# The experts' second product as three rounded products, with its operands split per tile on three engines

## The chip, the cores and the metric

One core of one Trainium2 chip runs the whole program. The metric is the time of one execution on the device in microseconds (us). A TensorE clock of 1.0 in the profile is its full 2.4 GHz.

## The reference, cut to what matters

The program computes two layers over 2 x 512 tokens of width 256. The first layer multiplies a selective scan with a mixture of experts, the second multiplies an attention with a layer of signs. The change is in the mixture of experts, whose reference is:

```
router = xt @ gate_w.T
probs, idx = jax.lax.top_k(router, K)          # K = 2 of E = 8 experts
for e in range(E):
    h = jax.nn.silu(xt @ fc1_w[e].T) * (xt @ fc2_w[e].T)    # 704 hidden units
    y = y + comb[:, e:e + 1] * (h @ proj_w[e].T)
```

The last line's product, `h @ proj_w[e].T`, is what the change makes in another way.

## The kernel before, in words

The 2048 pairs of a token and an expert are sorted by expert into NJ = 23 tiles of 128 rows, each for one expert. For tile j, GpSimd gathers the rows (`xg`), TensorE transposes them (`turn_x`, called X), ScalarE copies them to `xgT`. TensorE then makes the hidden values in three parts: H1 (the first product's 512 units, bank 0), H2 (the second product's, bank 1) and H3 (the remaining 192 of both, bank 2). ScalarE applies silu into `sil` after H1 and after H3; VectorE multiplies into `hE` (128 x 768, two buffers). `project(j)`, called P(j), then makes the tile's output from `hE` and the `proj_w` columns of `wm` (five blocks of 128 units) and `ptl` (the sixth), all in plain float32. VectorE scales the result by the router's weight into `y_row`, and GpSimd scatters that to DRAM. The hidden units are on the partitions, so P(j) sums six matmuls of 128 x 128 by 256 columns in bank 3.

Meanwhile the same engines run the selective scan in 8 chunks: F(c) on TensorE and two exponentials on ScalarE (`decays`), C(c) on TensorE, four copies `dx` on ScalarE (`skips`), products `mix` and `c_dec` on GpSimd (`mixes`), Y(c) on TensorE (`scan_back`), the state, `gate` and `y_lo` on VectorE, `y_hi` on ScalarE, and O(c) on TensorE (`out_rows`).

The order of both is written by hand in `side_by_side()`: a list of (place, engine, operation, number), sorted by place. Tile j has the places from 4j on, chunk c those from `CHUNK_AT[c]` = 3 + 11.5c. Each engine executes its operations strictly in that order and waits at the head of its queue on semaphores. So P(j-1) at place 4j + 3.1 stands between H3(j) and H1(j+1) on TensorE. SyncE loads the weights of a tile into one of three slots: `expert_rows(j)`, and `expert_back(j)` for the `proj_w` columns, which waits for P(j-3) to end.

The selective scan's last product in `out_rows` already has the form that the change brings to P(j): `split3` makes one product from three of type float32r (a rounded float32, here "the rounded format"): low part by high, high by low, high by high.

Of the kernel before, what the change touches and what calls it, by code (L numbers as in the profile page):

```python
# [175 lines left out]
def layered_kernel(nc, x, params, consts, select, rope, w_in, w_out, w_moe, w_moe_tail, w_qkv, w_o, w_sign, out):  # L176
# [4 lines left out]
    with ctx:  # L181
# [260 lines left out]
        wcen_ready, wsign_ready, sign_ready, sign_full, ab_ready, g1_ready, mask_ready, o_zero = sems(  # L442
            "wcen_ready wsign_ready sign_ready sign_full ab_ready g1_ready mask_ready o_zero")

        k_scaled, turns_full, turns_ready, rp4_ready, wqhi_done, wqlo_done, wohi_done, wolo_done, twice_in = sems(
            "k_scaled turns_full turns_ready rp4_ready wqhi_done wqlo_done wohi_done wolo_done twice_in")
# [228 lines left out]
        def _(dve):  # L675
# [270 lines left out]
            def centre_signs():  # L946

                dve.wait_ge(l1_in, 32)
                for i, (s, at) in enumerate(((0, 0), (1, 0), (1, HD // 2))):
# [4 lines left out]
                for m in range(KC):
                    TS(wcen[:, m, :], wsg[:, m, :], wst[:, m, 1:2], None, ALU.subtract).then_inc(wcen_ready, 1)
                TT(ab[:, :], cols("alpha"), cols("bias"), ALU.mult).then_inc(ab_ready, 1)
# [1073 lines left out]
```

## Time and profile before

| | |
|---|---|
| median of 3 runs | 753.35 us (749.12 to 753.63) |
| the profiled execution, its own time | 748.34 us |
| its span, first to last instruction | 746.5 us |
| mean granted TensorE clock | 0.993 |
| experts and scan side by side | about 66 to 299 us of the span |
| P(0) to P(22), records of L1734 | 276, from 79.3 to 296.8 us |

The page's first part gives each engine's busy time over the span. In the timeline, records of one line that follow each other are merged: `x10` are ten records, the number before the engine is the time from the first's start to the last's end. A float32 matmul is two records. A bracket tells how long the engine was idle before and who released it. Because matmuls are pipelined, the start of the next group is what tells when a group let go of the engine.

### The profile page before, as it was taken

How to read it: one execution, taken by the hardware profiler on the slowest of the kernel's cores; microseconds unless marked ns; L12 is line 12 of the kernel's file. 1: busy time of each engine (PE TensorE's matmuls, PEld its weight loads, DVE VectorE, ACT ScalarE, POOL GpSimd, SP SyncE). 2: the span in 40 equal slices, each digit the busy share in tenths (PEclk: the TensorE clock that was granted, in tenths of full speed). 3: DMA queues.
4: the chain of work that ended last, by engine and by line, in shares of the span. 5: the costliest groups of instructions: out<-in, count | busy, mean ns of one | idle time of the engine just before them, and what ended most of it. 6: DMA issues, size and time to landing. Idle time of an engine off the chain costs nothing.

```text
span 746.5 us, 13408 instructions
## 1 busy us (share of the span) xinstructions
PE 688.0 (92%) x4447; PEld 598.2 (80%) x4448; DVE 510.5 (68%) x1072; ACT 442.0 (59%) x1075; POOL 385.2 (52%) x434
## 2 busy tenths in 40 slices
PE   2999999999999999699879999999999999999976
PEld 2887998989889898587668888888888878787864
DVE  7483556434333245897878878888888888887765
ACT  4435343332341432448786787778877788878772
POOL 1403342432224312235765797777877788777540
PEclk9899999999999999999999999999999999999999
DMA  8165877787778755226533332343324423242011
GB/s 293 44 217 170 286 240 241 252 261 229 247 234 251 214 170 163 43 76 191 147 109 79 93 82 65 95 93 83 85 65 102 93 66 87 58 110 58 1 29 57
DMA packets 108453, 102.25 MB, mean 137 GB/s; under 512 B 51104, under 2 KB 78688, under 8 KB 108256
## 3 DMA queue, kind: packets, MB, share of 16 engines
q1 hardware_dynamic: 106272, 95.62, 44.8%
q0 software_dynamic: 2112, 5.77, 2.4%
q8 instruction: 36, 0.59, 0.3%
q14 instruction: 33, 0.27, 0.1%
HBM read 69.24 MB, written 11.14 MB: 108 GB/s over the span
## 4 chain that ended last, share of the span: by engine, by line
PE 65%; DVE 20%; ACT 6%; issue 5%; POOL 2%; DMA 1%; SPq 1%; DVEq 0%; ACTq 0%
PE bank L1700 14%; PE bank L1734 8%; PE bank L1556 7%; PE bank L1873 5%; DVE p_lo L1071 3%; PE bank L1840 3%; DVE o_rest L1080 3%; PE bank L1560 3%; DVE nmax L1062 3%; PE bank L1561 3%; PE bank L1562 3%; PE bank L1841 2%; DVE q_mix L1028 2%; DVE q_mix L1029 2%; PE bank L1884 2%
## 5 line engine op out<-in xcount | busy, mean ns | idle before, releaser
L1518 POOL TENSOR_TENSOR prob<-prob,rinv 128x128 f32<-128x128 f32 (+3 forms) x256 | 176.6, 722 | 89.2 <-DVE rinv L1067 89.2
L1322 ACT ACTIVATE prob<-bank,nmax 128x512 f32<-128x512 f32 (+3 forms) x256 | 133.2, 526 | 42.3 <-DVE nmax L1062 30.7
L1071 DVE TENSOR_TENSOR p_lo<-bank,p_hi 128x512 fp32r<-128x512 f32 x160 | 109.5, 685 | 58.0 <-ACT p_hi L1329 55.9
L1329 ACT ACTIVATE p_hi<-bank 128x512 fp32r<-128x512 f32 x160 | 95.4, 596 | 44.1 <-PE bank L1556 43.1
L1700 PEld LDWEIGHTS bank<-xgT,wm 128*128 128x128 f32 x920 | 108.7, 192 | 4.5 <-issue 2.9
L1700 PE MATMUL bank<-xgT,wm 128*128 128x128 f32 x920 | 111.3, 275 | 0.5 <-ACT xgT L1234 0.5
L1840 PE MATMUL bank<-kT,qT 128*128 128x512 f32 (+3 forms) x256 | 83.4, 331 | 19.8 <-ACT prob L1322 15.3
L1556 PE MATMUL bank<-cst,prob 128*128 128x128 f32 x640 | 96.6, 273 | 3.2 <-ACT prob L1322 2.5
L1062 DVE TENSOR_REDUCE nmax<-bank 128x1 f32<-128x512 f32 (+2 forms) x192 | 91.3, 502 | 2.8 <-PE bank L1843 2.6
L1873 PE MATMUL bank<-p_lo,v_parts 128*128 128x256 f32 (+3 forms) x288 | 91.7, 341 | 0.1
L1491 POOL DMA_INDIRECT y_rows<-y_row,to_row x21 | 22.8, 1084 | 118.2 <-DVE y_row L931 92.5
L1556 PEld LDWEIGHTS bank<-cst,prob 128*128 128x128 f32 x640 | 73.2, 141 | 5.2 <-ACT prob L1322 2.6
L1840 PEld LDWEIGHTS bank<-kT,qT 128*128 128x128 f32 x256 | 48.1, 188 | 33.9 <-ACT prob L1322 26.6
L1841 PE MATMUL bank<-kT,qT 128*128 128x512 f32 (+3 forms) x256 | 74.4, 321 | 0.0
L1873 PE MATMUL bank<-p_hi,v_parts 128*128 128x256 f32 (+3 forms) x288 | 74.2, 304 | 0.0
L1259 ACT ACTIVATE sil<-bank 128x512 f32<-128x512 f32 x23 | 13.7, 597 | 75.9 <-PE bank L1700 75.9
L971 DVE TENSOR_TENSOR hE<-sil,bank 128x512 f32<-128x512 f32 x23 | 15.8, 687 | 57.5 <-PE bank L1700 40.6
L1734 PE MATMUL bank<-wm,hE 128*128 128x256 f32 x230 | 53.5, 379 | 1.2 <-DVE y_low L936 1.2
L1873 PEld LDWEIGHTS bank<-p_lo,v_parts 128*128 128x128 f32 x288 | 52.1, 190 | 0.3 <-issue 0.3
L1873 PEld LDWEIGHTS bank<-p_hi,v_parts 128*128 128x128 f32 x288 | 52.4, 190 | 0.0
L1322 ACT ACTIVATION_READ_ACCUMULATOR prob<-bank,nmax 128x1 f32 x256 | 51.2, 200 | 0.0
L1841 PEld LDWEIGHTS bank<-kT,qT 128*128 128x128 f32 x256 | 48.2, 188 | 2.9
(310 smaller groups left out, 1517.9 us busy)
## 6 DMA issues: line engine op xcount, KB each, us to landing
wm<-in_w_moe SPq DMA_DIRECT2D x23, 1280.0 KB
wm<-in_w_moe SPq DMA_DIRECT2D x23, 640.0 KB, 5.1
qT<-q_hi SPq DMA_DIRECT2D x124, 64.0 KB, 2.0
qT<-q_lo SPq DMA_DIRECT2D x124, 64.0 KB, 2.0
wo_twice<-wo_hi SPq DMA_DIRECT2D x32, 128.0 KB, 2.5
k_exp<-k_rows SPq DMA_DIRECT2D x56, 64.0 KB, 2.0
wtl<-in_w_moe_tail SPq DMA_DIRECT2D x46, 64.0 KB
y_rows<-gate SPq DMA_DIRECT2D x1, 2048.0 KB, 13.8
```

Source lines behind the costliest of these rows:

```text
L1062: ins = vec.tensor_reduce(out=nmax[:, i % 2, h, j:j + 1], in_=bk[:, at:at + (j + 1) * P], op=ALU.max, axis=AX.X, negate=True)
L1071: TT(p_lo[:, b_, :], bank[2 + b_ % 2][:, :], p_hi[:, b_, :].bitcast(F32), ALU.subtract).then_inc(plo_done, 1)
L1322: ins = actv(prob[:, i % 2, h, POFF[j]:POFF[j] + (j + 1) * P], bk[:, at:at + (j + 1) * P], ACT.Exp, bias=nmax[:, i % 2, h, j:j + 1], accum ...
L1329: actv(p_hi[:, b_, :], bank[2 + b_ % 2][:, :], ACT.Copy).then_inc(phi_done, 1)
L1491: pool.indirect_dma_start(out=y_rows, out_offset=bass.IndirectOffsetOnAxis(ap=to_row[:, n:n + 1], axis=0), in_=y_row[:, n % 2, :], in_offs ...
L1518: ins = GT(seg, seg, rinv[:, i % 2, k, j:j + 1].to_broadcast([P, (j + 1) * P]), ALU.mult)
L1556: return nc.tensor.transpose(dst, src, ident)
L1700: ins = mm(dst, w(c), xgT[:, u, c, :], start=c == 0, stop=c == KC - 1)
L1734: ins = mm(bank[3][:, 0:C], hE[:, u, i * P:(i + 1) * P], wm[:, s, i, PJ:WM] if i < FULL else ptl[:, s, :], start=i == 0, stop=i == HC - 1)
L1840: mm(dst, qs, kT[:, b, 0, 0:n], start=(h, j, at) == SCORES[k][0], stop=False)
L1841: mm(dst, qs, kT[:, b, 1, 0:n], start=False, stop=False)
L1873: ins = mm(bank[4 + h][:, x:y], vs, p[:, b_, at + x - j * P:at + y - j * P], start=first and (h, j) in ((0, 0), (1, 2)), stop=end and (h, ...
```

## The change

P(j) is made of three products of the rounded format: low part of `hE` by high part of the weights, high by high, high by low. Four operations per tile are new:

- hU (ScalarE): `hE_hi`, the rounded copy of the tile's 128 x 768 `hE`. It waits until P(j-1) has ended, since `hE_hi` has one buffer.
- hL (VectorE): `hE_lo` = `hE` - `hE_hi`, 128 x 768.
- pU (ScalarE): `pj_hi`, the rounded copy of the tile's weights, 128 x 1280 and 128 x 256.
- pL (GpSimd): the low parts, written over the weights in `wm` (`wm_lo`), in pieces of 512, 512 and 256 columns, and `ptl_lo`, 256 columns.

`hE`, `hE_hi`, `hE_lo`, `pj_hi` and `ptl_lo` have one buffer each. Some semaphores are merged to make room for three new ones; each wait keeps its meaning.

```
+            z += [(at + 3.6, "ACT", "hU", j), (at + 3.7, "DVE", "hL", j), (at + 4.2, "ACT", "pU", j), (at + 4.3, "POOL", "pL", j)]
...
-                    if n > 1:
-                        dve.wait_ge(row_full, n - 1)
-                    TT(hE[:, u, 0:4 * P], sil[:, 0:4 * P], bank[1][:, :], ALU.mult).then_inc(hE_done, 1)
+                    if n > 0:
+                        dve.wait_ge(hlo_done, n)
+                    TT(hE[:, 0:4 * P], sil[:, 0:4 * P], bank[1][:, :], ALU.mult).then_inc(hE_done, 1)
...
+                elif op == "hL":
+                    dve.wait_ge(upper_done, 2 * n + 1)
+                    TT(hE_lo[:, :], hE[:, :], hE_hi[:, :].bitcast(F32), ALU.subtract).then_inc(hlo_done, 1)
...
+                elif op == "hU":
+                    act.wait_ge(hE_done, 2 * n + 2)
+                    if n == 0:
+                        act.wait_ge(ones_ready, 5)
+                    else:
+                        act.wait_ge(row_full, n)
+                    actv(hE_hi[:, :], hE[:, :], ACT.Copy).then_inc(upper_done, 1)
+                elif op == "pU":
+                    s = n % 3
+                    act.wait_ge(back_in[s], 32 * (n // 3 + 1))
+                    actv(pj_hi[:, 0:FULL, :], wm[:, s, :, PJ:WM], ACT.Copy)
+                    actv(pj_hi[:, FULL, :], ptl[:, s, :], ACT.Copy).then_inc(upper_done, 1)
...
+                elif op == "pL":
+                    s = n % 3
+                    gp_.wait_ge(upper_done, 2 * n + 2)
+                    for lo, hi in ((0, 2), (2, 4), (4, FULL)):
+                        GT(wm_lo[:, s, lo:hi, PJ:WM], wm[:, s, lo:hi, PJ:WM], pj_hi[:, lo:hi, :].bitcast(F32), ALU.subtract)
+                    GT(ptl_lo[:, :], ptl[:, s, :], pj_hi[:, FULL, :].bitcast(F32), ALU.subtract).then_inc(pjlo_done, 1)
...
+                pe.wait_ge(upper_done, 2 * j + 2)
+                pe.wait_ge(hlo_done, j + 1)
                 for i in range(HC):
-                    ins = mm(bank[3][:, 0:C], hE[:, u, i * P:(i + 1) * P], wm[:, s, i, PJ:WM] if i < FULL else ptl[:, s, :],
-                             start=i == 0, stop=i == HC - 1)
+                    ps = slice(i * P, (i + 1) * P)
+                    mm(bank[3][:, 0:C], hE_lo[:, ps], pj_hi[:, i, :], start=i == 0, stop=False)
+                    mm(bank[3][:, 0:C], hE_hi[:, ps], pj_hi[:, i, :], start=False, stop=False)
+                pe.wait_ge(pjlo_done, j + 1)
+                for i in range(HC):
+                    ins = mm(bank[3][:, 0:C], hE_hi[:, i * P:(i + 1) * P], wm_lo[:, s, i, PJ:WM] if i < FULL else ptl_lo[:, :],
+                             start=False, stop=i == HC - 1)
                 ins.then_inc(row_full, 1)
```

GpSimd's queue around tile 9, where chunk 3 asks for `mix` and `c_dec`. Before (the scatter of tile 7's rows, the gather for tile 12, the scatter of tile 8's, the gather for tile 13, then the scan):

```order
L1491 DMA y_rows<-y_row,to_row 4992x256
L1457 DMA xg<-xn_rows,from_row 128x256
L1491 DMA y_rows<-y_row,to_row 4992x256
L1457 DMA xg<-xn_rows,from_row 128x256
L1466 TENSOR_TENSOR mix<-within,cbm 128x512
L1468 TENSOR_TENSOR c_dec<-since,CT 128x512
```

The same place now, from the scatter of tile 8's rows on:

```order
L1521 DMA y_rows<-y_row,to_row 4992x256
L1481 DMA xg<-xn_rows,from_row 128x256
L1515 TENSOR_TENSOR wm_lo<-wm,pj_hi 128x2x256 x2
L1515 TENSOR_TENSOR wm_lo<-wm,pj_hi 128x256
L1516 TENSOR_TENSOR ptl_lo<-ptl,pj_hi 128x256
L1490 TENSOR_TENSOR mix<-within,cbm 128x512
L1492 TENSOR_TENSOR c_dec<-since,CT 128x512
```

The four subtractions pL(9) now stand ahead of the scan's two products. Chunks 0, 1 and 2 have the same order (pL of tiles 0, 3 and 6).

ScalarE's queue between the silu after H3(6) and the next tile, where chunk 2 has its exponentials and `dx`. Before:

```order
L1217 ACT_TABLE_LOAD
L1217 ACTIVATE within<-bank 128x512
L1218 ACTIVATE since<-bank 128x512
L1226 ACTIVATE dx<-xs,par 128x128 x4
L1259 ACT_TABLE_LOAD
L1259 ACTIVATE sil<-bank 128x512
L1234 ACTIVATE xgT<-bank 128x256
```

Now:

```order
L1229 ACT_TABLE_LOAD
L1229 ACTIVATE within<-bank 128x512
L1230 ACTIVATE since<-bank 128x512
L1284 ACTIVATE hE_hi<-hE 128x768
L1238 ACTIVATE dx<-xs,par 128x128 x4
L1271 ACT_TABLE_LOAD
L1271 ACTIVATE sil<-bank 128x512
L1288 ACTIVATE pj_hi<-wm 128x1280
L1289 ACTIVATE pj_hi<-ptl 128x256
L1246 ACTIVATE xgT<-bank 128x256
```

hU(6), which waits for P(5), now stands ahead of `dx`, the table load and the silu of H1(7), and pU(6) behind that silu.

TensorE's queue from the last third of P(6) on, now:

```order
L1771 MATMUL bank<-wm_lo,hE_hi 128x256 x5
L1771 MATMUL bank<-ptl_lo,hE_hi 128x256
L1696 MATMUL bank<-mix,x_dt 128x128
L1698 MATMUL bank<-c_dec,state 128x128
```

Y(2) (`mix`, `c_dec`) still follows P(6) at once, as before, and H1(8) stands behind it.

## Rows read from the trace of the kernel before

**Rows 1.** The page, part 1: busy time of each engine, share, count.
```profile
PE 688.0 (92%) x4447; PEld 598.2 (80%) x4448; DVE 510.5 (68%) x1072; ACT 442.0 (59%) x1075; POOL 385.2 (52%) x434
```
**Rows 2.** Tile hE: the line that scales each tile's result after P(j).
```profile
L931 DVE TENSOR_SCALAR y_row<-bank,tab x21: 475/484/484, 82.1 to 283.1; 128x256 f32<-128x256 f32 x21
```
**Rows 3.** Timeline (start, us, engine, line): P(8), H1(10), c_dec, Y(3), H1(11).
```profile
159.78 2.32 PE L1734 MATMUL bank<-wm,hE 128*128 128x256 f32 x10
...
162.38 1.95 PE L1700 MATMUL bank<-xgT,wm 128*128 128x128 f32 x16
...
166.87 1.28 POOL L1468 TENSOR_TENSOR c_dec<-since,CT 128x512 f32<-128x512 f32 x1
...
168.41 0.46 PE L1666 MATMUL bank<-mix,x_dt 128*128 128x128 f32 x2 [0.73 <-POOL c_dec L1468]
...
173.72 1.95 PE L1700 MATMUL bank<-xgT,wm 128*128 128x128 f32 x16
```
**Rows 4.** Timeline: O(0), twelve rounded matmuls of 256 columns, and what follows.
```profile
93.08 0.36 PE L1560 MATMUL bank<-w_out_hi,y_lo 128*128 128x256 f32 x1
93.28 0.28 PE L1561 MATMUL bank<-w_out_lo,y_hi 128*128 128x256 f32 x1
...
94.59 0.38 PE L1556 MATMUL bank<-cst,xg 128*128 128x128 f32 x2
```
**Rows 5.** Timeline of ACT: silu after H1(8), copies of 256, 512 and 1024 columns.
```profile
145.13 0.60 ACT L1259 ACTIVATE sil<-bank 128x512 f32<-128x512 f32 x1 [6.46 <-PE bank L1700]
145.62 0.38 ACT L1234 ACTIVATE xgT<-bank 128x256 f32<-128x256 f32 x1
145.89 0.63 ACT L1206 ACTIVATE y_hi<-gate 128x512 fp32r<-128x512 f32 x1
...
292.47 1.04 ACT L1252 ACTIVATE wv_hi<-wv 128x1024 fp32r<-128x1024 f32 x1
```
**Rows 6.** Timeline of POOL: two subtractions into the rounded format.
```profile
296.19 2.38 POOL L1483 TENSOR_TENSOR wv_lo<-wv,wv_hi 128x1024 fp32r<-128x1024 f32 x1 [11.34 <-DVE xs L985]
300.36 1.27 POOL L1486 TENSOR_TENSOR wk_lo<-wk,wk_hi 128x512 fp32r<-128x512 f32 x1 [1.80 <-DVE xs L985]
```
**Rows 7.** Timeline of PE: C(2), P(6), Y(2), H1(8), P(7).
```profile
132.12 0.38 PE L1649 MATMUL bank<-CT,BT 128*128 128x128 f32 x2
...
132.78 1.95 PE L1700 MATMUL bank<-xgT,wm 128*128 128x128 f32 x16
...
137.91 2.32 PE L1734 MATMUL bank<-wm,hE 128*128 128x256 f32 x10
...
140.50 0.38 PE L1666 MATMUL bank<-mix,x_dt 128*128 128x128 f32 x2
...
143.15 1.95 PE L1700 MATMUL bank<-xgT,wm 128*128 128x128 f32 x16
...
148.28 2.32 PE L1734 MATMUL bank<-wm,hE 128*128 128x256 f32 x10
```
**Rows 8.** Timeline of ACT: table load before a silu, and the four dx copies.
```profile
130.85 1.27 ACT L1226 ACTIVATE dx<-xs,par 128x128 f32<-128x128 f32 x4
132.14 1.28 ACT L1259 ACT_TABLE_LOAD   x1
```
**Rows 9.** Timeline: DVE after H3(0); PE when it lets go of P(0).
```profile
72.89 0.29 DVE L975 TENSOR_TENSOR hE<-sil,bank 64x128 f32<-64x128 f32 x1
...
81.90 1.95 PE L1700 MATMUL bank<-xgT,wm 128*128 128x128 f32 x16
```
**Rows 10.** Timeline of PE: the end of P(21), then P(22).
```profile
292.59 0.59 PE L1734 MATMUL bank<-ptl,hE 128*128 128x256 f32 x2
294.38 2.40 PE L1734 MATMUL bank<-wm,hE 128*128 128x256 f32 x10 [1.19 <-DVE y_low L936]
```
**Rows 11.** Timeline: a product on POOL and one on DVE that start together.
```profile
114.69 1.05 POOL L1447 TENSOR_TENSOR decay_in<-cst,dts 128x512 f32<-128x512 f32 x1
114.73 1.57 DVE L904 TENSOR_TENSOR state<-state,since 128x512 f32<-128x512 f32 x1 [0.92 <-PE bank L1668]
```

More of the change, by code:

```diff
@@ L196, in layered_kernel @@
         x_tok = sb("x_tok", [P, NT, C])
+        xnT_at = (nc.sbuf_base + 31) // 32 * 32
         xnT = sb("xnT", [P, KC, T])
@@ L264, in layered_kernel @@
         ssm = first("ssm", [P, NCH, TAPS - 1 + SEQ])
+        route_at = first.at
         route = first("route", [P, NT, E])
@@ L324, in layered_kernel @@
         rp4 = turns[:, :, :].rearrange("p i (t h d) -> p i t h d", t=TB, h=4)
+        idle = Map(xnT_at)
+        pj_hi = idle("pj_hi", [P, HC, C], F32R)
+        ptl_lo = idle("ptl_lo", [P, C], F32R)
+        hE_hi = Map(route_at)("hE_hi", [P, HC * P], F32R)
         tiles = Map(scan.at)
@@ L327, in layered_kernel @@
         sil = tiles("sil", [P, HC * P])
-        hE = tiles("hE", [P, 2, HC * P])
+        hE = tiles("hE", [P, HC * P])
+        hE_lo = tiles("hE_lo", [P, HC * P], F32R)
         y_row = tiles("y_row", [P, 2, C])
@@ L335, in layered_kernel @@
         ptl = weights("ptl", [P, 3, C])
+        wm_lo = Map(weights.at)("wm_lo", [P, 3, FULL, WM], F32R)
         wm = weights("wm", [P, 3, FULL, WM])
@@ L436, in layered_kernel @@
         row_out = [sem(f"row_out{i}") for i in range(2)]
-        pad_zero, xg_full, xgT_ready, hid_full, sil_done, hE_done, row_full, row_taken = sems(
-            "pad_zero xg_full xgT_ready hid_full sil_done hE_done row_full row_taken")
+        upper_done, hlo_done, pjlo_done, xg_full, xgT_ready, hid_full, sil_done, hE_done, row_full, row_taken = sems(
+            "upper_done hlo_done pjlo_done xg_full xgT_ready hid_full sil_done hE_done row_full row_taken")
         mixed, gated = sems("mixed gated")
         sg_ready, back_full, x_ready, q_first, second_ready = sems("sg_ready back_full x_ready q_first second_ready")
[L442 to L446, printed above, removed]
+        signs_ready, wsign_ready, sign_ready, sign_full, g1_ready, mask_ready, o_zero = sems(
+            "signs_ready wsign_ready sign_ready sign_full g1_ready mask_ready o_zero")
+        k_scaled, turns_full, turns_ready, wqhi_done, wqlo_done, wohi_done, wolo_done, twice_in = sems(
+            "k_scaled turns_full turns_ready wqhi_done wqlo_done wohi_done wolo_done twice_in")
         v_full, v_copied, kx_full, kx_roped, kadd_done, k_in, khi_done, klo_done, vhi_done, vlo_done = sems(
@@ L879, in _ @@
             dve.wait_ge(pr_full, len(PROJS))
-            vec.memset(hE[0:TAIL, :, FULL * P:HC * P], 0.0).then_inc(pad_zero, 1)
+            vec.memset(hE[0:TAIL, FULL * P:HC * P], 0.0).then_inc(ones_ready, 1)
             def scan_front(c):
@@ L954, in centre_signs @@
                 for m in range(KC):
[L955 to L956 removed]
+                    TS(wcen[:, m, :], wsg[:, m, :], wst[:, m, 1:2], None, ALU.subtract).then_inc(signs_ready, 1)
+                TT(ab[:, :], cols("alpha"), cols("bias"), ALU.mult).then_inc(signs_ready, 1)
             for engine, op, n in side_by_side():
@@ L1406, in _ @@
             act.sem_inc(exp_done, 2)
-            act.wait_ge(ab_ready, 1)
+            act.wait_ge(signs_ready, 3 + KC + 1)
             attend(0, schedule("first"))
@@ L1728, in project @@
                 if j == 0:
-                    pe.wait_ge(pad_zero, 2)
+                    pe.wait_ge(ones_ready, 5)
                 pe.wait_ge(xgT_ready, min(j + 3, NJ))
@@ L1776, in _ @@
             sum_pair(3)
-            pe.wait_ge(rp4_ready, 3)
+            pe.wait_ge(signs_ready, 3)
             for i in range(3):
```

12 lines of the change are left out of this document (6 added, 6 removed).

## The prediction

> **What bounds the kernel now.** The page's first part has TensorE busy for 92% of the span and no other engine above 68% [rows 1]. In the stretch with the experts its timeline has almost no bracket: P, H1, X, H2, H3 and the scan's pieces follow each other, and the one long wait among P(8) to H1(11) is 0.73 us for `c_dec` [rows 3]. So a microsecond less on TensorE is a microsecond less in all, as long as nobody makes TensorE wait. The 21 scaled tiles lie 201.0 us apart from first to last, 10.05 us a tile [rows 2]. The shortest period is tile 6's: from 132.12, when TensorE lets go of P(5), to 140.50, when it lets go of P(6), 8.38 us [rows 7]; tile 3 has the same. I call T(j) the moment at which TensorE lets go of P(j).
>
> **The matmuls: -8.7 us.** P(j) takes 162.38 - 159.78 = 2.60 us now [rows 3]. The new form has the pattern of O(0), rounded, 256 columns: twelve in 94.59 - 93.08 = 1.51 us, and behind the first 1.31 / 11 = 0.119 us each [rows 4]. So the first twelve take 1.51, the last six 0.71, together 2.22 us: 0.38 less per tile, 8.7 us for 23. Bounds: if each group of six pays the start again, 2.26 (7.8 us); if none does, 18 x 0.119 = 2.14 (10.6 us). This is all that the change can win.
>
> **The new chain.** hU(j) can't start before T(j-1). From there to T(j), in a tile with nothing in the way:
> - hU, 768 columns. ScalarE copies 256, 512 and 1024 columns in 0.38, 0.63 and 1.04 us and starts the next one some 0.1 us before the end [rows 5], so 768 take 0.82. From T(j-1) + 0.2, it is done at 1.0.
> - Next in its queue is the silu of H1(j+1), which needs TensorE's H1: in tile 8, H1 begins at 143.15 and the silu at 145.13, 1.98 later [rows 7, 5]. It gives way after 0.49.
> - pU: 1280 columns, 1.17 by the same slope, then 256, 0.38. Done at 1.98 + 0.49 + 1.55 = 4.02.
> - pL: GpSimd takes 1.27 for 512 and 2.38 for 1024 columns [rows 6], 0.0022 a column; 512, 512, 256, 256 take 1.24 + 1.24 + 0.68 + 0.71 = 3.87. With 0.08 to start, done at 7.97.
> - TensorE sees it 0.26 later (as `c_dec`, which ends at 166.87 + 1.28 = 168.15 for Y(3) at 168.41 [rows 3]) and makes the last six in 0.71: T(j) = T(j-1) + **8.95 us**.
>
> The weights are no part of it: they are asked for after P(j-3), two tiles earlier. hL, about 0.95, is done before pU.
>
> A tile with a period of over 9.33 (8.95 + 0.38) hides the chain and wins its 0.38; most do, at a mean of 10.05. These don't, worked out in order of the queues. "Loss" is against the period less 0.38:
> - **Tile 0, 3.2.** hU(0) waits for `hE` (73.18 [rows 9]) and stands ahead of chunk 0's table load and exponentials, so these end some 1.5 later; the silu of H1(1) comes at 77.75, pU at 78.2 to 79.8, pL until 83.75, the end of P(0) at 84.7 instead of 81.90.
> - **Tile 3, 1.2.** A table load of 1.28 [rows 8] behind hU moves the silu to 2.3: 9.25 against 8.00.
> - **Tile 6, 2.4.** hU to 1.0, the four `dx` to 2.2, the table load to 3.5 [rows 8], silu, pU to 5.5, pL to 9.4: 10.4 against 8.00.
> - **Tile 7, 3.4.** `mix` and `c_dec` stand behind pL(6) and are done 2.5 after it, at T(5) + 12.0. Y(2) follows P(6) at once [rows 7] and so waits 1.8. Y(2) takes 2.65 (140.50 to 143.15), H1(8) is behind it, and the whole chain behind H1(8): 1.8 + 2.65 + 8.95 = 13.4, against 10.37 - 0.38 = 9.99.
> - **Tile 9, 5.0.** hU, table load, silu and pU to 4.35, pL to 8.3, `mix` and `c_dec` to 10.8. Y(3) is due at T(8) + 5 and starts at 11.05; it takes 2.71, and P(9) 2.22 behind it: 16.0, against 173.72 - 162.38 - 0.38 = 10.96 [rows 3].
> - **Tiles 12, 15, 16, 19, 2.9 in all.** Worked out in the same way from their places in the timeline: GpSimd's scatter, `mix` and gather ahead of pL make the chain 9.35, 11.1 and 9.3 in tiles 12, 15, 16; in tile 19 `y_hi` stands ahead of hU, 10.3. Their periods less 0.38 are shorter by 0.3, 0.8, 0.6 and 1.2.
> - **Tile 22, 4.0.** Nothing but P(22) is left, so the chain stands free, without the H1: 0.2 + 0.82 + 1.55 + 0.08 + 3.87 + 0.26 + 0.71 = 7.5. Now 294.38 + 2.60 - (292.59 + 0.43) = 3.96 [rows 10], less 0.38 is 3.6.
> - **Collisions, 1.2.** A product of two SBUF tensors on VectorE that starts with one on GpSimd takes 1.57: until GpSimd's ends at 115.74, and 0.56 more [rows 11]. `y_lo` for O(3) and O(4) now meets pL; I take 0.6 for each.
>
> Sum of the losses 3.2 + 1.2 + 2.4 + 3.4 + 5.0 + 2.9 + 4.0 + 1.2 = 23.3; less 8.7 is **+14.6 us**. Behind the stage nothing hides it: the layer's sum needs P(22). Against the profiled execution's own 748.34 this is 763; against the median of 753.35 it is 768. The four known times lie in two pairs (748.3, 749.1; 753.4, 753.6), so I take **766**.
>
> A rule that speaks against the change: the Trainium skill, GPSIMD Engine Reference, section Key points, says that GpSimd contends with VectorE instructions of two SBUF inputs. By rows 11 that is one exclusion in a stretch; by the rule every one of hL, `y_lo`, the state's and the gate's products pays where it meets pL, and the sum would be that of the third case below.
>
> **The rivals.**
> 1. *The waits as worked out*: 0.60. Its own range, with the bounds of the matmuls and 20% on pL's length in eight places, is 758 to 775.
> 2. *A shorter chain.* If GpSimd's and ScalarE's copies of 128 x 1280 strided columns run 20% faster than the slope (it comes from two rows, rows 6), each of the eight losing places gives back about 0.9: +7, 757 to 762. 0.16. Against it: nothing in rows 5 or 6 is faster with more columns.
> 3. *The two engines exclude each other.* pL lasts 3.87 of each tile. Each chunk has three or four VectorE products of two SBUF tensors (`state`, `gate`, `y_lo`, and hL each tile); 8 chunks, each one such meeting of 0.9 in a chain that TensorE waits for: +7 more, 773 to 782. 0.15. Rows 11 speak for it, that most such products follow TensorE's and fall ahead of pL speaks against it.
> 4. *Faster.* The split ends before TensorE gets there, and the 8.7 stay: 742 to 748. The mechanism is the length of pL: the chain hides in the short tiles once it is below 8.00, so pL would have to be under 2.9 instead of 3.87, and for tile 9 it would have to end before T(8) + 2.4, where GpSimd hasn't yet the upper parts. The second can't be, so only the rest of it can. 0.09.
>
> A difference of 1% (7.5 us) is what can be told from none here. Above 760.9 lie all of the third case, nearly all of the first and a quarter of the second: slower 0.76; same 0.15; faster 0.09. The range for 8 in 10 is 755 to 778: it leaves out the fourth case, a bit of the low end and half of the third.
>
> **What would show it.** The rounded matmuls of P have starts 0.12 us apart. In most tiles P(j)'s second line waits for nobody; in tiles 0, 3, 6, 7, 22 TensorE idles before the line with `wm_lo`, with `ptl_lo`'s subtraction as releaser, and before Y(2) and Y(3) with `c_dec` as releaser, about 1.8 and 6 us. T(9) - T(8) is 16 instead of 11.3, T(22) - T(21) 7.5. pL is four operations of 3.9 us in all. The attention behind it keeps its length. I am wrong if pL takes clearly less, if the chain's start isn't T(j-1), or if VectorE's products stretch to 1.5 us by the dozen.

## The result and the profile after

The changed kernel takes **789.38 us** (median of 4 runs, 787.44 to 793.58) against 753.49 us of the kernel before in the same comparison. It is slower: the two medians stand 4.8% apart, and the ratio on record is 1.054 (95% interval 1.050 to 1.058). I had forecast slower, at 766 us, with a range from 755 to 778. The direction was right; the size was 23 us short. The profiled execution took 793.58 us, its span is 791.8 us.

The page's first part, which answers to [rows 1]:

```profile
PE 698.4 (88%) x4585; PEld 610.3 (77%) x4586; DVE 553.8 (70%) x1095; ACT 492.8 (62%) x1144; POOL 482.6 (61%) x526
```

TensorE's busy time went up by 10 us, although it has less to do: a busy microsecond is worth less where the clock is halved. The line that scales each tile's result starts 233.9 us apart from first to last, where it was 201.0 [rows 2]:

```profile
L940 DVE TENSOR_SCALAR y_row<-bank,tab x21: 472/484/485, 85.0 to 318.9; 128x256 f32<-128x256 f32 x21
```

TensorE lets go of P(22) at 336.8 us instead of 297.0, so 39.8 of the 45.3 us of span lie in this stage. (The two profiled executions are further apart than the medians, which differ by 36 us.) The rest lies behind the stage, which I had expected to keep its length: 455.0 us after T(22) instead of 449.5, with the same matmuls, at a mean granted clock of 0.98 instead of 1.00. In the traces of the experiments below it is 451 to 455 us, so most of this is a difference between single executions. Tile by tile (T(j) - T(j-1), in us; the others differ by at most 0.7 from before):

| tile | before | forecast | after |
|---|---|---|---|
| 0, T itself | 81.9 | 84.7 | 84.8 |
| 1 | 9.5 | 9.1 | 9.2 |
| **2** | 11.1 | 10.7 | **18.5** |
| 3 | 8.4 | 9.25 | 9.4 |
| 4 | 10.4 | 10.0 | 11.1 |
| 5 | 10.9 | 10.5 | 12.4 |
| 6 and 7 | 18.6 | 23.8 | 27.3 |
| 8 | 11.7 | 11.3 | 12.6 |
| 9 | 11.3 | 16.0 | 18.4 |
| 15 | 10.7 | 11.1 | 12.5 |
| **19** | 9.45 | 10.3 | **13.6** |
| 22, from T(21) | 4.0 | 7.5 | 8.9 |

**The matmuls and the chain are as worked out.** P(1) at the high clock, twelve and then six at a pitch of 0.12 us (columns: start, us from the first's start to the last's end, engine, line, what is written and read):

```profile
91.62 0.36 PE L1767 MATMUL bank<-pj_hi,hE_lo 128*128 128x256 f32 x1
91.82 0.28 PE L1768 MATMUL bank<-pj_hi,hE_hi 128*128 128x256 f32 x1
91.94 0.28 PE L1767 MATMUL bank<-pj_hi,hE_lo 128*128 128x256 f32 x1
...
93.17 0.85 PE L1771 MATMUL bank<-wm_lo,hE_hi 128*128 128x256 f32 x5
...
93.99 1.94 PE L1730 MATMUL bank<-xgT,wm 128*128 128x128 f32 x16
```

ScalarE's part behind T(3) = 121.83: hU 0.84 (estimate 0.82), the silu of H1(4) 1.98 behind T(3), pU 1.26 and 0.41 (estimates 1.17 and 0.38), done at T + 4.0:

```profile
122.08 0.84 ACT L1284 ACTIVATE hE_hi<-hE 128x768 fp32r<-128x768 f32 x1 [2.75 <-PE bank L1771]
123.81 0.60 ACT L1271 ACTIVATE sil<-bank 128x512 f32<-128x512 f32 x1 [0.88 <-PE bank L1730]
124.30 1.26 ACT L1288 ACTIVATE pj_hi<-wm 128x1280 fp32r<-128x1280 f32 x1
125.46 0.41 ACT L1289 ACTIVATE pj_hi<-ptl 128x256 fp32r<-128x256 f32 x1
```

**What was not in the sum: VectorE stands still beside pL.** VectorE and GpSimd around T(1) and in tile 2:

```profile
91.94 0.68 DVE L920 TENSOR_TENSOR dx<-bank,dx 128x512 f32<-128x512 f32 x1
92.65 2.77 DVE L921 TENSOR_TENSOR gate<-dx,gate 128x512 f32<-128x512 f32 x1
...
97.82 6.76 DVE L874 SCALAR_TENSOR_TENSOR xs<-ssm,par,xs 128x512 f32<-128x512 f32 x3
```
```profile
92.39 0.73 POOL L1516 TENSOR_TENSOR ptl_lo<-ptl,pj_hi 128x256 fp32r<-128x256 f32 x1
93.09 1.03 POOL L1471 TENSOR_TENSOR decay_in<-cst,dts 128x512 f32<-128x512 f32 x1
94.11 0.76 POOL L1458 TENSOR_SCALAR xs<-ssm,par 128x512 f32<-128x512 f32 x1
...
99.44 3.17 POOL L1515 TENSOR_TENSOR wm_lo<-wm,pj_hi 128x512 fp32r<-128x512 f32 x3
102.58 0.71 POOL L1516 TENSOR_TENSOR ptl_lo<-ptl,pj_hi 128x256 fp32r<-128x256 f32 x1
103.28 0.76 POOL L1458 TENSOR_SCALAR xs<-ssm,par 128x512 f32<-128x512 f32 x1
```

The gate product starts at 92.65 and ends at 95.42, which is 0.55 behind the end of GpSimd's *third* instruction in a row (94.11 + 0.76 = 94.87), not behind the one that it met. The taps' three products end at 104.58, again 0.54 behind the end of GpSimd's unbroken run (104.04); without a meeting they take 2.31 together. In [rows 11] I had read the same 0.56 behind a single instruction and priced a meeting by one instruction. `dx`, which reads PSUM, keeps its 0.68 while pL runs. Not every meeting lasts to the run's end. Beside runs of two or more GpSimd instructions, 14 VectorE instructions of the stage were stretched: three lasted to the end (this gate, the first tap, and the gate at 129.34 us) and took 10.1 us more than the same instructions elsewhere, eleven ended within the run and took 8.5 us more. In all, 20 instructions took 23.3 us more up to T(22), 13 of them 1.5 us or longer; in the kernel before it was two, with 1.1 us. That is the last sign that I had named ("stretch to 1.5 us by the dozen"). H2(3)'s and the residual's operations stand behind the taps in VectorE's queue, and TensorE behind those:

```profile
105.78 2.05 PE L1671 MATMUL bank<-decay_in,cst 128*128 128x512 f32 x2 [3.60 <-DVE sT L931]
107.62 1.91 PE L1672 MATMUL bank<-decay_in,ones 128*128 128x512 f32 x2
...
109.55 0.42 PE L1768 MATMUL bank<-pj_hi,hE_hi 128*128 128x256 f32 x1
109.76 0.41 PE L1767 MATMUL bank<-pj_hi,hE_lo 128*128 128x256 f32 x1
```

**And the clock.** Behind that wait the pitch is 0.21 instead of 0.12 us: TensorE runs at the lower of its two levels, 1.2 instead of 2.4 GHz. Busy time of the engines in stretches of the stage (the number before the last two is the granted clock, as a share of full speed):

```profile
core 0: us, PE busy (x) PEld busy (x) DVE busy (x) ACT busy (x) POOL busy (x), PEclk, DMA share, GB/s
66.00:102.00 36.00, 31.57 (x254) 29.21 (x253) 19.78 (x28) 19.28 (x39) 21.49 (x22) 1.00 0.71 218
102.00:113.00 11.00, 7.40 (x29) 5.19 (x28) 4.51 (x6) 3.71 (x7) 2.04 (x3) 0.69 0.42 131
...
191.00:204.00 13.00, 6.78 (x41) 6.34 (x42) 3.08 (x5) 0.24 (x2) 5.96 (x5) 0.74 0.35 113
204.00:301.00 97.00, 89.36 (x720) 83.03 (x718) 50.52 (x83) 52.89 (x96) 69.33 (x65) 1.00 0.75 235
...
328.00:338.00 10.00, 5.53 (x25) 5.25 (x25) 5.65 (x8) 4.34 (x7) 7.16 (x5) 0.60 0.37 122
```

The kernel before had 1.00 in the whole stretch from 66 to 300. Summed over short stretches up to T(22), TensorE's busy time times (1 - granted clock) is 11.7 us; I call this the low clock's share.

TensorE's waits up to T(22) (us in total, how often, the longest):

```profile
PE bank L1771 <- POOL ptl_lo L1516: 10.6, 9, 1.9
PE bank L1696 <- POOL c_dec L1492: 9.4, 3, 6.8
PE bank L1590 <- DVE y_lo L926: 7.5, 5, 2.6
PE bank L1671 <- DVE sT L931: 3.6, 1, 3.6
PE bank L1767 <- ACT pj_hi L1289: 2.7, 1, 2.7
```

All idle brackets of TensorE from 66 us to T(22) add up to 38.1 us; before, to 2.9. So the books nearly close: 38.1 - 2.9 + 11.7 - 8.7 = 38.2, against the 39.8 us by which T(22) is later. For the runs below the same sum, each with its own gain from the matmuls, holds within 1 us, except in e10 (1.8) and e5 (3.6) and where waits are filled, if it is counted from each run's own start of the stage: in ten of them (e3 to e7, v1 to v3, e9 and e12) this lies 1.6 to 2.0 us earlier, because less low clock stands ahead of it, so that their T(22) in the table flatters them by that much.

### The profile page after: what moved, and what is told of

It is laid out like the page before. It is cut to its first block, busy times and chain, and to the rows that moved or that the text cites. A ratio compares the mean times of both kernels' runs of the same rounds, so it can differ in the third digit from the quotient of the medians.

```text
span 791.8 us, 13914 instructions
## 1 busy us (share of the span) xinstructions
PE 698.4 (88%) x4585; PEld 610.3 (77%) x4586; DVE 553.8 (70%) x1095; ACT 492.8 (62%) x1144; POOL 482.6 (61%) x526
## 4 chain that ended last, share of the span: by engine, by line
PE 47%; DVE 24%; POOL 12%; issue 9%; ACT 6%; DMA 1%; SPq 1%; DVEq 0%; ACTq 0%; POOLq 0%
PE bank L1586 6%; PE bank L1730 5%; POOL wm_lo L1515 5%; PE bank L1910 5%; DVE p_lo L1083 3%; PE bank L1877 3%; PE bank L1590 3%; DVE o_rest L1092 3%; PE bank L1592 3%; PE bank L1591 3%; DVE nmax L1074 3%; PE bank L1878 2%; DVE q_mix L1040 2%; DVE q_mix L1041 2%; PE bank L1921 2%
## 5 line engine op out<-in xcount | busy, mean ns | idle before, releaser
L1730 PE MATMUL bank<-xgT,wm 128*128 128x128 f32 x920 | 112.9, 278 | 0.5 <-ACT xgT L1246 0.5
L1515 POOL TENSOR_TENSOR wm_lo<-wm,pj_hi 128x512 fp32r<-128x512 f32 (+1 forms) x69 | 77.9, 1158 | 38.0 <-ACT pj_hi L1289 37.9
L1521 POOL DMA_INDIRECT y_rows<-y_row,to_row x21 | 24.7, 1176 | 53.1 <-DVE y_row L940 49.9
L1284 ACT ACTIVATE hE_hi<-hE 128x768 fp32r<-128x768 f32 x23 | 19.3, 841 | 58.3 <-PE bank L1771 53.5
L1092 DVE SCALAR_TENSOR_TENSOR o_rest<-o_hi,minus,bank 128x512 fp32r<-128x512 f32 x64 | 47.1, 736 | 1.0 <-ACT o_hi L1365 1.0
```

Of the source, the lines that this page charges most:

```text
L1092: STT(out=to, in0=o_hi[:, b, m, :].bitcast(F32), scalar=minus[:, k:k + 1], in1=bank[4 + k][:, :], op0=ALU.mult, op1=ALU.add).then_inc(olo_ ...
L1515: GT(wm_lo[:, s, lo:hi, PJ:WM], wm[:, s, lo:hi, PJ:WM], pj_hi[:, lo:hi, :].bitcast(F32), ALU.subtract)
L1730: ins = mm(dst, w(c), xgT[:, u, c, :], start=c == 0, stop=c == KC - 1)
```

## The experiments

Three theories of the missing 23 us. **A, the exclusion:** VectorE's products stop beside pL, up to as long as GpSimd's run lasts, and TensorE behind them. **B, the length:** pL's time in the chain and in GpSimd's queue costs more than worked out. **C, the clock:** what TensorE's low clock costs, and whether it comes from TensorE's own waits or from the load beside it. The texts on record word their theories B and C for each run anew. Each ratio is to the kernel before, run with it on the same chip (748 to 750 us), with its 95% interval.

| run | us | ratio | T(22) | TensorE idle | low clock |
|---|---|---|---|---|---|
| before | 749 | | 297.0 | 2.9 | 0 |
| after | 789.4 | 1.054 | 336.8 | 38.1 | 11.7 |
| e1_low_on_dve | 785.5 | 1.048 (1.039 to 1.056) | 330.9 | 35.0 | 10.8 |
| e2_low_behind_scan | 790.7 | 1.055 (1.049 to 1.061) | 337.5 | 39.3 | 12.4 |
| e3_no_low_weights | 733.7 | 0.981 (0.976 to 0.987) | 280.0 | 12.9 | 0 |
| e4_before_plus_subtractions | 767.3 | 1.022 (1.015 to 1.029) | 311.5 | 14.6 | 3.4 |
| e5_one_operand | 800.0 | 1.068 (1.061 to 1.074) | 343.0 | 43.1 | 12.6 |
| e6_before_plus_one_operand | 767.7 | 1.024 (1.019 to 1.030) | 311.1 | 13.2 | 4.9 |
| v1_parts_first | 804.3 | 1.073 (1.067 to 1.079) | 347.3 | 45.8 | 17.6 |
| v2_parts_first_on_dve | 774.8 | 1.034 (1.028 to 1.040) | 319.3 | 28.7 | 7.1 |
| e7_tiny_memsets | 754.5 | 1.009 (1.007 to 1.012) | 300.2 | 14.6 | 2.6 |
| e8_before_plus_tiny_memsets | 751.0 | 1.004 (1.002 to 1.006) | 299.4 | 4.2 | 1.7 |
| e9_waits_filled | 792.3 | 1.058 (1.055 to 1.061) | 337.6 | | 2.6 |
| **e10_116_memsets** | 772.3 | 1.028 (1.022 to 1.034) | 318.0 | 26.2 | 5.0 |
| **e11_before_plus_116_memsets** | 756.6 | 1.009 (1.007 to 1.012) | 305.4 | 8.2 | 2.7 |
| e12_half_the_filling | 783.3 | 1.045 (1.040 to 1.050) | 328.7 | 24.7 | 3.4 |
| v3_out_later | 771.3 | 1.029 (1.024 to 1.034) | 318.1 | 27.3 | 7.1 |

### First four: the parts of the change

**e1_low_on_dve**, pL on VectorE:

```
-            z += [... (at + 4.3, "POOL", "pL", j)]
+            z += [... (at + 4.3, "DVE", "pL", j)]
```

> The changed kernel with the four subtractions of pL made by VectorE, at the same place in the order. Theory A, the exclusion: most of the 27 us by which the stage came out longer than worked out is VectorE standing still while GpSimd runs pL (gate's, taps' and xs' products of 2.8, 6.8 and 4.2 us), and what the half clock of TensorE costs behind such a stop. With GpSimd out of it no product of VectorE lasts longer than before the change, the chain gets shorter by some 2 us (VectorE does the four in about 1.9 us instead of 3.9) and mix and c_dec come as early as before: 750 to 765. Theory B, the chain itself with its queue on ScalarE: only the 2 us of the chain in the eight losing tiles come back, 770 to 780. Theory C, VectorE has no room for 23 x 1.9 us more in front of H2 and state: 775 or more, with VectorE named as releaser before H3 and Y.

785.5 us. The gate and `y_lo` are short again, but pL now waits for pU on VectorE at T + 4 with everything of the chunk behind it: TensorE waited 17.9 us for `y_lo` in seven places instead of 7.5 in five. Nor is the exclusion gone: pL's own subtractions, now on VectorE, met GpSimd's products of the scan (up to 2.52 us instead of 0.68, beside `mix` and `c_dec`). One cause had taken the place of another, so this run could not tell A from B; its own theory C (no room on VectorE, 775 or more) had the time, though TensorE waited before O and not before H3 and Y.

**e2_low_behind_scan**, pL at 4j + 6.1, behind `mix` and `c_dec`:

> The changed kernel with pL at place 4j+6.1 instead of 4j+4.3, so that in GpSimd's queue mix and c_dec of a chunk stand ahead of it. Theory A, the exclusion: the 1.7 and 6.8 us before Y(2) and Y(3) go, and what the low clock behind them costs, but pL still runs 4.2 us per tile beside VectorE and its products still stop, and P's last six wait longer in the tiles where mix is ahead: 778 to 792. Theory B, the order in GpSimd's queue is where the loss came from: 765 to 775.

790.7 us. The waits before Y fell from 9.4 to 1.6 us and came back before the last six matmuls (17.0) and before O (11.5). So a change of the order in GpSimd's queue alone gives nothing back.

**e3_no_low_weights**, no pL and no last six matmuls:

> The changed kernel without pL and without the last six matmuls of each P (the products with the weights' lower parts are left out). hU, hL and pU stay. The matmuls alone are 23 x 0.71 = 16.3 us less than in the changed kernel and 23 x 1.09 = 25 less than before. Theory A, the exclusion: no wait of more than a microsecond is left, 730 to 742. Theory B, the copies on ScalarE (2.4 us per tile ahead of exponentials and silus) carry a good part of the loss: 755 or more, with TensorE idle before H2, H3 or F for ScalarE.

733.7 us, 15 below before, where the matmuls alone are 25 less. hU, hL and pU thus cost about 10 us: idle time rose by about 10 us, of it 3.5 before O and 2.7 in tile 22 for `pj_hi`. The rest of the change's loss hangs on pL.

**e4_before_plus_subtractions**, the kernel before with pL's work beside it and nobody waiting for it:

```
+                    for lo, hi in ((0, 512), (512, 1024), (1024, 1280), (1280, 1536)):
+                        ins = GT(spare_low[:, lo:hi], x_flat[:, lo:hi], x_flat[:, lo + 256:hi + 256], ALU.subtract)
```

> The kernel before, and beside it four subtractions of GpSimd per tile at pL's place, of pL's sizes (512, 512, 256, 256 columns of float32, two SBUF operands, other data and an unused area), started by the silu of H1(j+1); nobody waits for them before the stage's end, so only the time they take on GpSimd and in its memory port is added. Theory A, the exclusion: VectorE's products stop behind them as in the changed kernel and TensorE behind VectorE, and mix and c_dec come later: 762 to 780, with single gate, taps or state products of 2 us and more. Theory B, it is the new chain (P waits for the parts) that costs: 753 to 758.

767.3 us: 18 to 19 us only because GpSimd is busy. The gate products took 1.27 us in the mean and `y_lo` 1.41 (before 0.72 and 0.69), and TensorE waited for both engines:

```profile
PE bank L1572 <- DVE y_lo L921: 6.8, 4, 3.6
PE bank L1678 <- POOL c_dec L1473: 6.1, 2, 4.5
```

That refutes the chain's half of theory B, since this kernel has no chain through pL. What GpSimd's queue costs by itself is told by e11 below: 7 of these 19 us.

### Second four: one operand, and another order

**e5_one_operand** and **e6_before_plus_one_operand**:

```
-  GT(wm_lo[...], wm[...], pj_hi[...], ALU.subtract)
+  pool.tensor_scalar(wm_lo[...], wm[...], w, b, ALU.mult, ALU.add)
```

> The changed kernel with pL as ten scalings of one SBUF operand each (256 or 128 columns by a scalar per partition, two of the 256 written to an unused area) that should take 3.6 to 4.0 us together, as its four subtractions do; the lower parts of the weights are thus replaced by scaled copies. The places, the waits and the queue are the same; only the second operand is gone. Theory A, the exclusion: VectorE's gate, taps, xs and y_lo keep their 0.7 us, the idle times before O (y_lo) and H2 (sT) go, and with them some of the low clock: 768 to 780. Theory B, pL's length and place in the queues alone: 785 to 793.

> The kernel before, and beside it per tile five scalings of 512 columns with one SBUF operand on GpSimd at pL's place (3.9 us together), where e4_before_plus_subtractions had four subtractions with two. Theory A, the exclusion: the 6.8 us of waiting for y_lo of that run go and what is left is mix and c_dec behind the new work, 6 us and less: 753 to 760. Theory B, GpSimd's time in the queue alone costs the 19 us of that run: 764 to 770.

Both misses for theory A (e6 fell in the range of its theory B). e5 did not hold pL's length: a scaling of 256 columns took 0.57 us, one of 128 up to 0.51, so pL had 5.3 us instead of 4.1, and the wait before the last six went from 10.6 to 25.3 us. It can't be read for or against A. e6 did hold it (0.80 us each) and cost the same as e4. Its trace shows why: one SBUF operand on GpSimd's side is enough. VectorE, then GpSimd:

```profile
186.31 4.20 DVE L923 TENSOR_TENSOR y_lo<-gate,y_hi 128x512 fp32r<-128x512 f32 x1
```
```profile
185.20 0.77 POOL L1499 TENSOR_SCALAR spare_too<-x_tok,par 128x512 fp32r<-128x512 f32 x1
185.95 3.00 POOL L1501 TENSOR_SCALAR spare_low<-x_tok,par 128x512 fp32r<-128x512 f32 x4
188.93 1.03 POOL L1454 TENSOR_TENSOR decay_in<-cst,dts 128x512 f32<-128x512 f32 x1
```

`y_lo` ends at 190.51, GpSimd's run of six instructions at 189.96: 0.55 apart again. Only my idea that the second operand of GpSimd matters fell.

**v1_parts_first**, pU ahead of the silu, hU behind it, `mix` ahead of pL:

```
+            z += [(at + 4.2, "ACT", "hU", j), (at + 4.3, "DVE", "hL", j), (at + 3.6 if j else 0.5, "ACT", "pU", j),
+                  ({0: 0.6, 3: 17.6, 6: 29.1, 9: 40.6}.get(j, at + 4.15), "POOL", "pL", j)]
```

> The changed kernel with another order: pU ahead of the silu of H1(j+1) and hU behind it, pL at 4j+4.15, tile 0's pU and pL already behind H1(0), and mix and c_dec of chunks 1 to 3 ahead of pL(3), pL(6) and pL(9). The chain from T(j-1) to T(j) is 0.2 + 1.55 + 0.08 + 3.87 + 0.26 + 0.71 = 6.7 instead of 8.95 us. If the chain and the queue are the greater part of the loss (10.6 us before wm_lo, 9.4 before Y, 3.2 in tile 0), 764 to 772 with almost no low clock left. If the exclusion and what the clock makes of it are, 776 to 788, since pL's 4.2 us beside VectorE stay.

804.3 us, the slowest of all, and worse than both expectations. The shorter chain starts pL while hU is still to come, so that hL meets pL in 13 of the 23 tiles:

```profile
L989 DVE TENSOR_TENSOR hE_lo<-hE,hE_hi 128x768 fp32r<-128x768 f32 x22 | 54.6, 2481 | 46.9 <-ACT hE_hi L1283 46.8
L875 DVE SCALAR_TENSOR_TENSOR xs<-ssm,par,xs 128x512 f32<-128x512 f32 x12 | 20.5, 1709 | 0.3
```

hL takes 2.48 us in the mean (0.95 alone), the taps 1.71 (0.75). TensorE waited 19.8 us for `y_lo` and 9.0 for `hE_lo`.

**v2_parts_first_on_dve**, the same with pL on VectorE:

> The order of v1_parts_first and pL on VectorE, ahead of hL. e1_low_on_dve had VectorE waiting for pU at T+4 with H2's product, state and y_lo behind it (17.9 us before y_lo); here pU is done at T+1.8, pL at T+3.7, hL at T+4.7, before H2's product is due. No exclusion, no late mix, no late silu: 745 to 757. Rival: VectorE, busy for 26 of 40 us then, still comes late with y_lo and state in the chunks: 765 or more.

774.8 us, so the rival: with pL and hL ahead of it `y_lo` is late (15.3 us in seven places). The exclusion that I had called gone is there too, in another place: gate, taps and `y_lo` keep their length, but the subtractions themselves have two SBUF operands and wait for GpSimd's `mix`, `c_dec` and `decay_in`. Twelve of them took 17 us more than alone. VectorE (the three take about 1.6 us alone), then GpSimd:

```profile
172.00 4.33 DVE L994 TENSOR_TENSOR wm_lo<-wm,pj_hi 128x512 fp32r<-128x512 f32 x3
```
```profile
173.54 1.28 POOL L1497 TENSOR_TENSOR mix<-within,cbm 128x512 f32<-128x512 f32 x1
174.77 1.26 POOL L1499 TENSOR_TENSOR c_dec<-since,CT 128x512 f32<-128x512 f32 x1
```

### Third: the length without long instructions

**e7_tiny_memsets** (where P's last six matmuls read `pj_hi`, so the low parts of the weights are left out) and **e8_before_plus_tiny_memsets**:

```
+                    for i in range(42):
+                        ins = pool.memset(unused[:, i:i + 1], 0.0)
+                    ins.then_inc(pjlo_done, 1)
```

> The changed kernel with pL as 42 memsets of 128 x 1 on GpSimd (0.10 us each where the trace has one alone, so about 4 us), and P's last six matmuls with the upper parts of the weights again (so the lower parts of the weights are left out). Queue, place and waits of pL stay and so does its length, but no instruction of it is longer than 0.1 us, so that VectorE can get in at any moment. Theory A, the exclusion (VectorE's products behind a long instruction or an unbroken run of GpSimd's are the idle times before O, 7.5 us, before tile 2's F, 3.6, and part of the low clock): gate, taps, y_lo and xs at 0.7 us, 770 to 778. Theory B, pL's length in chain and queue: 785 to 795. The run with one operand could not tell this, since its ten scalings took 5.4 us instead of 4.

> The kernel before, and beside it 42 memsets of 128 x 1 per tile on GpSimd at pL's place. Runs with four subtractions or five scalings there both came out 18 to 19 us over before, with gate and y_lo of VectorE at 1.25 us. Theory A: what VectorE loses there is the exclusion, by any long GpSimd instruction with one operand or two; with tiny ones only mix and c_dec are late (6 us of waits): 755 to 761. Theory B, queue occupancy alone: 765 to 770.

754.5 and 751.0 us, both below the expectation, since 42 memsets took 1.45 us in a row, not 4. They say something else: even with a pL of 1.45 us and no exclusion beside it the new form isn't faster than before.

**e10_116_memsets** and **e11_before_plus_116_memsets**, the same with 116:

> e7_tiny_memsets once more with 116 memsets instead of 42, since these took 0.034 us each and 1.45 together: 116 take 3.95 us, as pL's four subtractions do by themselves. The chain, the queue and the waits are thus those of the changed kernel, and no GpSimd instruction of pL is long. The lower parts of the weights are left out. Theory A, the exclusion: 767 to 775, with gate, taps, xs and y_lo at 0.7 us, no idle before tile 2's F, and the waits before the last six and before Y(2) and Y(3) that I had worked out (chain and queue), since what is left is the case that I had forecast, 766. Theory B, pL's length in chain and queue alone: 785 to 793.

> The kernel before with 116 memsets per tile on GpSimd at pL's place, 3.95 us that nobody waits for. With subtractions there it was 19 us slower, of which its trace had 6.1 us of waits for c_dec, 6.8 for y_lo and 3 of low clock. Theory A, the exclusion: the waits for c_dec stay and those for y_lo go: 755 to 760. Theory B, GpSimd's time alone: 765 to 770.

Both as theory A has it. 116 memsets take 3.8 to 3.9 us, pL's own length. e10 is 17 us below the changed kernel, and VectorE's gate and taps are back at their old means (total us, mean ns). `y_lo` is so only in part, 0.90 us (0.69 before, 1.05 in the changed kernel), because it also meets `decay_in` and GpSimd's tap:

```profile
L875 DVE SCALAR_TENSOR_TENSOR xs<-ssm,par,xs 128x512 f32<-128x512 f32 x12 | 9.0, 750 | 1.0 <-POOL xs L1459 0.7
L922 DVE TENSOR_TENSOR gate<-dx,gate 128x512 f32<-128x512 f32 x8 | 5.5, 692 | 0.3
```

In the changed kernel the same two were:

```profile
L874 DVE SCALAR_TENSOR_TENSOR xs<-ssm,par,xs 128x512 f32<-128x512 f32 x12 | 13.4, 1120 | 1.0 <-POOL xs L1458 0.7
L921 DVE TENSOR_TENSOR gate<-dx,gate 128x512 f32<-128x512 f32 x8 | 11.1, 1393 | 0.3
```

TensorE's waits in e10:

```profile
PE bank L1771 <- POOL unused L1515: 9.2, 9, 1.9
PE bank L1696 <- POOL c_dec L1493: 8.4, 3, 5.8
PE bank L1767 <- ACT pj_hi L1290: 2.7, 1, 2.7
PE bank L1590 <- DVE y_lo L927: 2.4, 2, 1.5
```

The chain's and the queue's waits are nearly as in the changed kernel (17.6 us instead of 20.0); the 3.6 us for `sT` are gone and those for `y_lo` fell from 7.5 to 2.4. Many tiles are those of the forecast: 10.7 in tile 2, 9.3 in tile 3, 10.4 in tile 5. Tiles 6 and 7 (25.6 instead of 23.8) and tile 9 (18.5 instead of 16.0) are longer than the forecast here too, so what they have above it isn't the exclusion beside pL. In e11 the same `y_lo` that took 4.20 us beside the scalings takes 0.68 in the middle of the memsets. VectorE, then GpSimd:

```profile
186.99 0.68 DVE L921 TENSOR_TENSOR y_lo<-gate,y_hi 128x512 fp32r<-128x512 f32 x1
```
```profile
185.78 3.78 POOL L1497 MEMSET spare_low<- 128x1 f32 x116
```

A memset reads nothing and is short, and these runs don't tell which of the two lets VectorE through. Nor does it let everything through: a copy `turns`, which took 0.41 us alone, took 2.26 us beside e10's memsets and 1.52 beside e11's, and ended 0.28 us behind each run. Of e4's 19 us, e11 keeps 7; TensorE's waits for `c_dec` are the same in both (6.1 and 5.8 us), so the other 12 come with the subtractions and not with GpSimd's time.

### The clock

**e9_waits_filled** and **e12_half_the_filling**, useless matmuls ahead of TensorE's longest waits (e9: 28, 48, 18, 20 and 12 of them; e12, shown here at the second place: 14, 27, 9, 8 and 6):

```
+                if c == 3:
+                    fill(27, 2 * 10 + 1)
                 pe.wait_ge(mix_ready, c + 1)
```

> The changed kernel with useless matmuls (128x128, float32, 0.12 us each at the high clock) in the waits of TensorE that stand before its low clock: 28 before chunk 1's F, 48 before Y(3), 18 before O(6), 20 before P(22) and 12 before its last six. If the half clock (12.1 us of busy time lost, by the windows of its trace) follows from TensorE standing idle, it stays at 2.4 GHz in tiles 2, 9, 20 and 22, and 6 to 8 us come back: 780 to 785. If it comes from the load of the other engines, the time is as before or longer by what the filling overshoots: 789 to 793.

> e9_waits_filled with half the filling, since each filling matmul was two passes of 0.118 us and the filling ran on for 2.8 us after chunk 1's F could have begun, and about 4 after Y(3) could: 14, 27, 9, 8 and 6 now. With the high clock F(1) to P(2) took 3.8 us there instead of 6.7, Y(3) to P(9) 4.8 instead of 6.3. If that is what the clock costs and nothing else is behind, 782 to 786; if the chain behind (the silu and pL of the next tile) sets the end whatever the clock is, 788 to 792.

e9 came out at 792.3 us: the filling ran on beyond the waits, because each of its float32 matmuls is two records of 0.12 us. Yet tile 2 took 18.1 us there instead of 18.5, although the filling ended about 2.5 us late: F(1) to the end of P(2) took 3.8 us at the high clock and 6.7 at the low one. With half of it, e12, 783.3 us: 6 us less than the changed kernel (the ratios' intervals only just meet; from each run's own start of the stage to T(22) it is 6.3 us), by nothing but matmuls that nobody needs. Three stretches of e12, around tiles 2, 9 and 22:

```profile
96.00:113.00 17.00, 16.49 (x136) 15.37 (x135) 12.63 (x16) 9.57 (x17) 8.80 (x10) 1.00 0.63 197
186.00:204.00 18.00, 16.02 (x136) 15.19 (x134) 8.48 (x13) 4.67 (x10) 11.03 (x10) 1.00 0.43 138
318.00:330.00 12.00, 9.40 (x80) 9.04 (x79) 8.04 (x13) 5.48 (x9) 8.14 (x7) 1.00 0.57 176
```

So in these stretches the low clock followed from TensorE's own idle time, not from the load beside it. Of the low clock's share of 11.7 us e12 removed 8.3, and 6 of them showed in the time; that the rest falls where another wait follows anyway is my reading and wasn't tested. Idle time isn't all that comes before a low clock: in the kernel before, the granted clock also fell to half at 26.0 us, while TensorE was busy with matmuls of 8 columns each and had not waited more than 0.5 us at a time since 13.3 us.

### Can the order give it back?

**v3_out_later**, v2 with O(c) 1.1 places later:

```
-        o = a + (9.5 if c + 1 < NT else 12.7)
+        o = a + (10.6 if c + 1 < NT else 12.7)
```

> v2_parts_first_on_dve (774.8 us) with the scan's O(c) 1.1 places later, at a + 10.6, so that TensorE has a product of a tile more to do before it needs y_lo. In that run the waits for y_lo were 15.3 us in seven chunks, up to 3.4 each. If they only came from O standing too early in TensorE's order, 760 to 766; if VectorE is late by as much as its load of 26 in 40 us makes it, the wait turns up again before H2, H3 or the next F: 770 to 776.

771.3 us. The wait for `y_lo` fell from 15.3 to 3.0 us and turned up again before P (`hE_lo`, 11.6 instead of 7.3) and before F (`sT`, 6.5 instead of 2.0): it is VectorE's load, with the stretched subtractions in it, not O's place. None of the versions tried beats the kernel before. As an estimate, the best that a hidden pL could give is e3 and the last six matmuls, 733.7 + 16.3 = 750 us, no better than before.

## Why the prediction was right and where it was wrong

- **Matmuls, -8.7: right.** P(1)'s first twelve took 1.50 us and its last six 0.82, against 1.51 and 0.71 worked out; in P(2), where the parts were there in time, the last six took 0.71.
- **The new chain, 8.95: right.** Tile 3 took 9.36 us against 9.25 worked out, T(0) came at 84.82 against 84.7. pL's own four operations took 3.9 us where nothing met them, 4.1 in the mean, up to 4.8 in tiles 9, 10 and 22.
- **The queue (tiles 7 and 9): right in place.** `c_dec` was the releaser before Y(2) and Y(3), with 1.69 and 6.78 us, where I had 1.8 and 6.
- **"Collisions, 1.2": the step that failed.** The mechanism was there, the term was mis-sized. The changed kernel without pL's part of it (e10) is at 772.3 us, so it costs 17 us: TensorE waits 11.9 us less there, ten times the 1.2, and the low clock's share is 6.7 us less. Of the 11.9, 8.7 are waits for VectorE (`y_lo`, `sT`) and 2.4 waits for GpSimd, whose pL is itself longer where VectorE comes in between. I had priced two meetings at 0.6 us each, from one row in which GpSimd had a single instruction [rows 11]. Two things were wrong with that. A meeting can last until the end of GpSimd's whole unbroken run, and pL makes runs of 4 to 6 instructions, with `decay_in` and the tap behind it: up to 4.45 us in tile 2 (6.76 instead of 2.31). And I counted only `y_lo`; gate, the taps, the state's product and the copies for `turns` pay beside pL too, and hL, which I hadn't counted either, beside `mix`, `c_dec` and `decay_in` (3.7 us in five tiles). The third rival named the mechanism and had 7 us more, at 0.9 a meeting, 773 to 782; it was the nearest and still too small, since it too had one price for every meeting and no low clock. The Trainium skill (GPSIMD Engine Reference, section Key points) says that GpSimd contends with VectorE instructions of two SBUF inputs. The traces agree on who is hit: gate 1.39 us in the mean, 0.72 before, `dx` with its PSUM operand 0.68; hit as well is the copy `turns`, which has one SBUF operand (0.95 to 1.96 us instead of 0.41). The page has no price for it; the runs do.
- **The low clock: a term that I didn't have.** I took every wait at its length. e10 is the case that I had worked out, but for the collisions with pL. Without these the forecast was 22.1 us of waits more than the 2.9 of before, 25.0 in all; e10 has 26.2. So the waits were right in sum, though in part by luck, since tiles 6, 7 and 9 were longer and others shorter than worked out. On top of that comes e10's low clock, 5.0 us: with it the forecast would have been 771, and e10's four runs lie at 767 to 774. Part of this agreement is the base: 766 stood between the two pairs of the kernel before, while the one beside e10 took 749.4, so e10 is 22.9 us above it where I had 14.6, and about 3 us stay open. The low clock could have been read from the trace of before, though not in this stage, whose longest wait was 1.2 us: right behind the stage TensorE waits 5.7 us until 313.3 us, and the granted clock is at half from 312.8 to 316.2.
- **The rival "faster": right to be small, for another reason.** I had written that the gain shows in the short tiles once pL is shorter than 2.9 us, and never in tile 9. e7's pL took 1.45 us, and the kernel 0.9% more than before. Tile 9 still waited 3.4 us for `c_dec`, as written; but what I hadn't priced is that hU, pU and hL cost about 10 us by themselves (e3), as much as the matmuls give.

The two together, 17 and 5 us, are 22 of the 23 us between 766 and 789. What stays open: why some meetings last to the end of the run and others don't; and whether VectorE would get through between short GpSimd instructions that do read SBUF. In e5, with pieces of 128 and 256 columns, gate and taps kept 0.70 and 0.75 us but `state`'s product took 1.36 and `y_lo` 0.97 in the mean, and one `state` 3.86 us across eight scalings of about 0.5 us. A change with gaps between pL's four pieces wasn't tried.

## What to carry to other kernels

Work that moves to GpSimd is not free because its queue is empty: for each run of consecutive GpSimd instructions on SBUF, list the VectorE instructions with two SBUF operands that may start in it, and charge each with up to the rest of the run and 0.55 us (the worst case; three of 14 meetings here came to it), then ask who waits for VectorE. Moving the work to VectorE doesn't avoid this where GpSimd has other products of its own (v2). To test such a suspicion, run the kernel before with the idle work beside it (e4), and the changed kernel with a stand-in of the same length that doesn't stop VectorE's products (e10). A wait of TensorE of a few microseconds can cost more than its length, since what follows it may run at half the clock (F(1) to the end of P(2): 6.7 us instead of 3.8).
